# Gated cross-attention block with a mixture of experts: a matrix conversion put ahead of the register reads, pair weights and a bias put elsewhere

## The reference, cut to what matters

```python
x = x + tanh(g_ffn[0]) * ffn(layernorm(x))
# ffn, with normed = rmsnorm(...) * norm_weight
shared = relu(normed @ sw1 + sb1) @ sw2 + sb2          # 256 -> 1024 -> 256
probs = sigmoid(flat @ router_w.T)                     # 8 experts
scores, idx = top_k(probs, 2)
w = scores / (sum(scores) + 1e-6)
h = relu(einsum("td,edh->teh", flat, ew1) + eb1)       # 8 experts, same widths
eo = einsum("teh,eho->teo", h, ew2) + eb2
routed = einsum("teo,te->to", eo, comb)                # comb holds w at idx
return shared + routed
```

## Time and profile before

| | |
|---|---|
| median of 3 runs | 702.06 us (701.38 to 702.97) |
| the profiled execution, whole | 701.34 us |
| its span | 699.5 us |
| TensorE busy in matmuls | 598.9 us, 86% of the span |
| VectorE busy | 482.4 us, 69% |
| ScalarE busy | 392.8 us, 56% |
| GpSimd busy | 281.7 us, 40% |

### The profile page before, as it was taken

How to read it: one execution, slowest core, us unless ns; L and a number is a source line. 1 busy time by engine, 2 the same in 40 slices (tenths; PEclk the granted TensorE clock), 3 DMA queues, 4 the chain that set the end, 5 groups by cost and what they waited for, 6 DMA issues and landing times. The chain is left out here.

```text
span 699.5 us, 19174 instructions
## 1 busy us (share of the span) xinstructions
PE 598.9 (86%) x6150; PEld 499.4 (71%) x6150; DVE 482.4 (69%) x1298; ACT 392.8 (56%) x994; POOL 281.7 (40%) x327
## 2 busy tenths in 40 slices
PE   2689999999999999999757999898999999799960
PEld 2457777777777778777536887787788788587850
DVE  6858777877777877778695766547555556556537
ACT  4368888888888888887716423144352444424320
POOL 7303444443443334446530178605345525355120
PEclk9799999999999999999975999999999999999995
DMA  8536557775555555632040042203434332341218
GB/s 219 153 81 144 151 138 188 184 197 135 132 130 137 138 141 138 155 87 68 1 181 1 9 152 84 98 23 116 141 110 147 107 120 91 120 138 46 61 49 311
DMA packets 86601, 84.29 MB, mean 121 GB/s; under 512 B 17879, under 2 KB 80341, under 8 KB 86430
## 3 DMA queue, kind: packets, MB, share of 16 engines
q1 hardware_dynamic: 78686, 70.83, 36.8%
q0 software_dynamic: 2976, 8.16, 3.2%
q10 hardware_dynamic: 4896, 4.76, 2.5%
HBM read 55.43 MB, written 28.30 MB: 120 GB/s over the span
## 5 line engine op out<-in xcount | busy, mean ns | idle before, releaser
L925 PE MATMUL ps<-ident,probs 112*125 112x112 f32 x768 | 192.6, 277 | 2.5 <-POOL probs L508 1.4
L713 ACT ACTIVATE probs<-probs,negmax 112x375 f32<-112x375 f32 x256 | 154.9, 608 | 26.0 <-DVE negmax L1227 25.8
L1079 PE MATMUL ps<-w,arena 128*128 128x256 f16 x1152 | 139.0, 277 | 20.8 <-DVE arena L1370 20.6
L763 ACT ACTIVATE arena<-ps,b 128x256 f32<-128x256 f32 x192 | 78.5, 473 | 138.8 <-PE ps L1068 138.8
L925 PEld LDWEIGHTS ps<-ident,probs 112*125 112x125 f32 x768 | 138.9, 188 | 23.6 <-issue 7.4
L1227 DVE CUSTOM_DVE_ANT_0 probs<-ps,neg 112x375 f32<-112x375 f32 x256 | 137.3, 538 | 11.8 <-issue 9.5
L1079 PEld LDWEIGHTS ps<-w,arena 128*128 128x128 f16 x1152 | 109.9, 99 | 45.6 <-DVE arena L1370 32.2
L508 POOL TENSOR_TENSOR probs<-probs,gp_in 112x375 f32<-112x375 f32 x64 | 58.6, 915 | 181.2 <-ACT probs L713 181.1
L1234 DVE TENSOR_TENSOR arena<-ps,gpT 125x336 f32<-125x336 f32 x192 | 97.0, 506 | 46.3 <-PE ps L925 45.7
L1068 PE MATMUL ps<-probs,w 128*128 128x256 f16 x816 | 91.9, 273 | 0.0
L1068 PEld LDWEIGHTS ps<-probs,w 128*128 128x128 f16 x816 | 79.9, 98 | 9.2
(11 more groups left out here) (173 smaller groups left out, 829.8 us busy)
## 6 DMA issues: line engine op xcount, KB each, us to landing
k_scratch<-kT SPq DMA_DIRECT2D x96, 93.8 KB
kst<-k_scratch SPq DMA_DIRECT2D x64, 140.6 KB, 3.5
w1s<-in_L_ffn_ew_dram SPq DMA_DIRECT2D x8, 1024.0 KB, 4.9
w2s<-in_L_ffn_ew_dram SPq DMA_DIRECT2D x8, 1024.0 KB, 5.6
x_sent<-y_sb SPq DMA_DIRECT2D x12, 516.0 KB, 5.1
ctx_in<-in_ctx_dram SPq DMA_DIRECT2D x16, 375.0 KB
probs<-x_sent ACTq DMA_DIRECT2D x18, 258.0 KB, 2.6
arena<-y_back SPq DMA_DIRECT2D x7, 512.0 KB, 7.1
```

The lines of the kernel that those rows point to most:

```text
L713: act.activation(probs[:, n % PROBS], probs[:, n % PROBS], ACT.Exp, bias=negmax[:, p, n:n + 1], scale=-1.0, accum_out=rowsum[:, p, ORDER[n ...
L763: act.activation(hid32[:, f], ps[:, f // 2 % 4, f % 2 * TILE:(f % 2 + 1) * TILE], ACT.Relu, bias=b1[:, f, e:e + 1]).then_inc(h_relu, 1)
L925: mm = pe.transpose(ps[0:KP, PT[n % 2], c * S:(c + 1) * S], probs[:, n % PROBS, c * KP:(c + 1) * KP], ident[0:S, 0:S])
L1079: mm = pe.matmul(ps[:, 4 + a, 0:D], hid[:, u, f, a * P:(a + 1) * P], w2[:, p, w, f], start=(f == 0 and j == 0), stop=(f == NF - 1 and j == 2))
```

## The change

Three edits. In the experts' loops of ScalarE and VectorE the conversion of the next first matrix comes ahead of the register read; the start of an expert is taken from the register that held the end of the one before, so each of these two engines reads one register for each expert instead of two, and one more at the very start. TensorE and GpSimd read as before. The seven instructions for the pair weights go from the end of the shared expert to the place behind its tile 2 (`weigh_pairs`), and ScalarE's exponential from behind tile 6 to behind tile 1. The bias `sb2` is added in each shared tile, to its own 256 rows, between the split and the wait for the result, with a wait of VectorE for its own addition (`sb2_added`).

```diff
--- before.py
+++ after.py
@@ -203,6 +203,7 @@
             sem("cnt_made"), sem("rank_mm"), sem("slot_made"), sem("tiles_made"), sem("scattered"))
         in_w1, in_w2 = sem("in_w1"), sem("in_w2")
         in_b2 = sem("in_b2")
+        sb2_added = sem("sb2_added")
         w1_hi, w1_lo, w2_hi, w2_lo = sem("w1_hi"), sem("w1_lo"), sem("w2_hi"), sem("w2_lo")
         x_in = sem("x_in")
         xT_mm, xT_made = sem("xT_mm"), sem("xT_made")
@@ -773,19 +774,21 @@
 
             activate(0, E)
             split_high(1, 1)
-            with act.Fori(1, ST) as i:
-                activate(i, E)
+            activate(1, E)
             act.wait_ge(dve_ask, 4)
             act.activation(top[:, 6:8], top[:, 6:8], ACT.Exp, scale=-1.0).then_inc(act_gave, 1)
+            with act.Fori(2, ST) as i:
+                activate(i, E)
             take_tile(0)
             act.wait_ge(words_taken, 1)
             load_tile(1)
             act.wait_ge(tiles_made, 1)
+            end = act.value_load(tile_of[0:1, 0:1], min_val=0, max_val=RT)
             for e in range(E):
-                first = act.value_load(tile_of[0:1, e:e + 1], min_val=e, max_val=RT)
-                end = act.value_load(tile_of[0:1, e + 1:e + 2], min_val=e + 1, max_val=RT)
+                first = end
                 if e + 1 < E:
                     split_high(e + 2, e % 2)
+                end = act.value_load(tile_of[0:1, e + 1:e + 2], min_val=e + 1, max_val=RT)
                 with act.Fori(first, end) as r:
                     activate(r + ST, e)
                     take_tile(r + 1)
@@ -1377,11 +1380,25 @@
             def shared_tile(i):
 
                 split_hidden(i)
+                two = bass.ds(2 * i, 2)
+                dve.tensor_tensor(x_sb[:, two], x_sb[:, two], sb2_bc[:, :].unsqueeze(1).to_broadcast([P, 2, D]), ALU.add).then_inc(sb2_added, 1)
+                dve.wait_ge(sb2_added, i + 1)
                 for a in range(TILE // P):
                     dve.wait_ge(y_mm, 2 * i + a + 1)
                     row = bass.ds(2 * i + a, 1)
                     dve.scalar_tensor_tensor(x_sb[:, row].rearrange("p a d -> p (a d)"), ps[:, 4 + a, 0:D], gates[:, 1:2],
                                              x_sb[:, row].rearrange("p a d -> p (a d)"), ALU.mult, ALU.add).then_inc(y_made, 1)
+
+            def weigh_pairs():
+
+                dve.wait_ge(act_gave, 5)
+                then(dve.tensor_scalar(top[:, 6:8], top[:, 6:8], 1.0, None, ALU.add))
+                then(dve.reciprocal(top[:, 6:8], top[:, 6:8]))
+                then(dve.tensor_tensor(top[:, 8], top[:, 6], top[:, 7], ALU.add))
+                then(dve.tensor_scalar(top[:, 8], top[:, 8], 1e-6, None, ALU.add))
+                then(dve.reciprocal(top[:, 9], top[:, 8]))
+                then(dve.tensor_scalar(top[:, 9], top[:, 9], gates[:, 1:2], None, ALU.mult))
+                then(dve.tensor_tensor(top[:, 6:8], top[:, 6:8], top[:, 9].unsqueeze(1).to_broadcast([P, 2, NT]), ALU.mult))
 
             then(dve.tensor_scalar(sb2_bc[:, :], sb2_bc[:, :], gates[:, 1:2], None, ALU.mult))
             shared_tile(0)
@@ -1389,21 +1406,10 @@
             shared_tile(1)
             split_up_low(1, 1)
             shared_tile(2)
-
-            dve.wait_ge(y_made, 2 * 3 + 2)
-            then(dve.tensor_tensor(x_sb[:, :, :], x_sb[:, :, :], sb2_bc[:, :].unsqueeze(1).to_broadcast([P, NT, D]), ALU.add))
+            weigh_pairs()
             with dve.Fori(3, ST) as i:
                 shared_tile(i)
 
-            dve.wait_ge(act_gave, 5)
-            then(dve.tensor_scalar(top[:, 6:8], top[:, 6:8], 1.0, None, ALU.add))
-            then(dve.reciprocal(top[:, 6:8], top[:, 6:8]))
-            then(dve.tensor_tensor(top[:, 8], top[:, 6], top[:, 7], ALU.add))
-            then(dve.tensor_scalar(top[:, 8], top[:, 8], 1e-6, None, ALU.add))
-            then(dve.reciprocal(top[:, 9], top[:, 8]))
-            then(dve.tensor_scalar(top[:, 9], top[:, 9], gates[:, 1:2], None, ALU.mult))
-            then(dve.tensor_tensor(top[:, 6:8], top[:, 6:8], top[:, 9].unsqueeze(1).to_broadcast([P, 2, NT]), ALU.mult))
-
             dve.wait_ge(z_done, 16 * ZEROS)
             dve.wait_ge(in_b2, 16)
 
@@ -1414,11 +1420,12 @@
 
             take_words(0)
             dve.wait_ge(tiles_made, 1)
+            end = dve.value_load(tile_of[0:1, 0:1], min_val=0, max_val=RT)
             for e in range(E):
-                first = dve.value_load(tile_of[0:1, e:e + 1], min_val=e, max_val=RT)
-                end = dve.value_load(tile_of[0:1, e + 1:e + 2], min_val=e + 1, max_val=RT)
+                first = end
                 if e + 1 < E:
                     split_up_low(e + 2, e % 2)
+                end = dve.value_load(tile_of[0:1, e + 1:e + 2], min_val=e + 1, max_val=RT)
                 with dve.Fori(first, end) as r:
                     split_hidden(r + ST)
                     dve.wait_ge(words_taken, r + 1)
```

## The result

Median of 19 runs 699.66 us (696.65 to 701.92), against 702.06 us of 19 runs of the kernel before on the same chip (701.10 to 705.79): 2.4 us less, ratio 0.9957, 95% interval 0.9942 to 0.9972. The forecast was 694.2, with a range from 689.5 to 699.0, and the measured time lies outside it. The profiled execution took 701.35 us, 1.7 more than the median. That of the kernel before took 701.34, so the two traces show none of the gain that the median has.

A forecast was written before the change was run, and what follows sets the result against it. TensorE was taken as the bound, so only its idle time could be won, with the engines' ring setting the time in places. 701.34 - 2.9 (shared stage) - 5.0 (experts) = 693.4, forecast 694.2 on the median's scale; range 689.5 to 699.0.

The forecast's parts named there:

- The bias tile by tile: Shared expert, VectorE: each bias piece takes 0.7 us, hidden in 0.92 us of idle time waiting for TensorE.
- Expert 0's high half: ScalarE's first matrix conversion starts 2.3 us sooner from earlier row words and one read less, besides the shared stage's 2.9.
- Reads: Experts 1 to 6: the high half no longer waits for two register reads, 1.09 us sooner at each expert.
- the rival of reads that wait: Reads wait for their engine's running instruction, so 0.5 to 0.6 us come back per expert: 697.7 us, chance 0.06.
- the one that the order gives nothing: Something else fills the 1.27 us before the high half; only shared stage and 1.75 us stay: 697.4, chance 0.03.
- Tile 5: Shared stage: GpSimd freed sooner, so VectorE's split overlaps its matrix conversion in fewer slow pairs, 1.1 us less loss.
- the likeliest case: One scatter held, at expert 2: 694.2 us, own range 692.3 to 696.3, chance 0.40.
- the slower cases: All scatters held (704.2 us, chance 0.06) and half of something unseen (0.05); slower together given 0.07.
- My central case is one held scatter, at expert 2: GpSimd's second scatter held by VectorE's low half costs 2.8 + 1.1 us; the experts' lead ends at 5.0 us.
- two or three held, about 697, up to 700: Rival: more than one expert's scatter held, each further one costing about 3 us of the lead; chance 0.16.
- Expert 4 adds 1.1, because its low half and the load behind it are early: At expert 4, already held before the change, the high half's lead grows by 1.1 us.
- None held: Rival: no scatter held by a low half; shared stage gives 2.9 and experts 8.8, 690.4 us, chance 0.24.

The follow-up runs named there:

- the reads alone: Kernel before with only the expert loops' register reads moved behind the matrix; two runs, 716.03 us (ratio 0.9994) and 705.46 us (1.0015).
- cut and later load: Changed kernel with w1's low half made by four instructions and the next 1 MB load held behind the conversion's first cut: 686.84 us, ratio 0.9767.
- The shared part alone: Changed kernel with register reads as in the kernel before; three runs: 720.95, 718.60 and 696.91 us, ratios 1.0139, 1.0118 and 0.9904.
- the fill: Changed kernel with ScalarE's one read kept ahead of its matrix and 14 unused matmuls in TensorE's gap in expert 0: 695.42 us, ratio 0.9890.
- later load, second run: Changed kernel with the next expert's 1 MB load held behind the first cut of GpSimd's conversion, on a disturbed chip: 709.10 us, ratio 0.9994.
- third run: Changed kernel with the next expert's 1 MB load held behind the first cut of GpSimd's conversion, on an undisturbed chip: 687.91 us, ratio 0.9792.

## Why the prediction was wrong

**Right, by its own steps.** The bias tile by tile: 0.68 to 0.71 us in idle time, forecast 0.7 at no cost. The weights: 1.72 us (418.15 to 419.87) in the pause. Tile 3: 1.80 us back. Expert 0's high half 5.1 us earlier, forecast 2.9 + 2.3. Reads: 1.08 us at each expert, forecast 1.09, with nothing waiting for them; the rival of reads that wait is out, and so is the one that the order gives nothing (the high half did come forward by the two reads). Tile 5 gave 0.8 and not 1.1, so the shared stage 2.7 and not 2.9. One bound was added up wrongly: the shared stage's 0.9 to 3.6 us give 693.5 to 696.2 for the likeliest case, not 692.3 to 696.3. And the chances of the slower cases add up to 0.085, not 0.07.

**Wrong: the step "My central case is one held scatter, at expert 2".** It counted two ties, experts 1 and 5, as going well, and let the hold at 2 set expert 3 free. The runs showed the opposite order, for a reason that I had half in hand. Behind a hold, ring and scatters move together, and the distance is that of expert 5 before, 1.08 us, less the 1.08 of the reads: +0.01 to +0.02 us at experts 2 and 5, in the change's two profiles and in both of the reads alone. The scatter was never held there. Behind an expert *without* a hold, TensorE sets the scatter, and the low half comes first. That is expert 1 (behind 0) and expert 3 (behind 2). The change's first profile shows who is waited for ahead of the scatters of experts 1 and 2: VectorE's last piece of `y_sb` waits for TensorE's matmuls at 1, and at 2 VectorE waits for GpSimd's landing (line 616) before it writes `dest`:

```profile
488.68 0.42 DVE L1441 TENSOR_TENSOR y_sb<-ps,kst 128x256 f32<-128x256 f32 x1 [0.71 <-PE ps L1082]
...
515.04 0.16 DVE L1434 SCALAR_TENSOR_TENSOR dest<-words 128x2 int32<-128x2 f32 x1 [4.75 <-POOLq L616]
```

So holds come at every second expert, two and not one: the rival "two or three held, about 697, up to 700", to which I gave 0.16. The size of one was near. The lead fell by 6.1 + 1.1 - 2.7 = 4.5 at the first and 3.7 + 1.1 - 1.5 = 3.3 at the second, forecast 2.8 + 1.1 = 3.9. That the mean is 3.9 too is luck: the conversion came 3.3 and 3.4 us late, not 2.8, and the further 1.1 came at the first only, since expert 3 has three tiles.

**Wrong: "Expert 4 adds 1.1, because its low half and the load behind it are early".** It took 1.9. The early low half was ahead of the first scatter too, so the first was held, the second came behind it, and both landed beside the load, and the conversion came 12.04 us and not 9.48 behind the low half. I had written that nothing of this hurts at expert 4, and took the cost of its hold as fixed. Sum on the traces: 7.9 forecast, less 3.9 for the second hold and 3.0 for expert 4, leaves 1.0; 0.4 was left. The rest is pieces of 0.1 to 0.2, the hold at expert 6 among them, which the prediction did not see.

**Only argued, or open.** At expert 1 the clock seems to decide how far the low half is ahead. In seven traces with the change's shared part and its reads, TensorE had a gap of 1.70 to 1.92 us in expert 0. In three its granted clock then fell to half (the change twice, cut and later load), and the low half was 0.98 to 0.78 us ahead. In four it did not, and the low half was between 0.21 us ahead and 0.01 behind. The shared part alone goes the same way: with a gap of 2.26 us each time, the low half was 0.94 and 0.99 us behind the scatter in the two traces whose clock stayed up, and 0.28 in the one whose clock fell. One trace with the fill supports it as a cause; why the clock falls in one execution and not in another stays open. Open too is why the median gained 2.4 us where the profiled execution gained nothing; I had no trace of a faster execution of this kernel. "None held", forecast 690.4, didn't occur by itself; with the landings moved out of the load's way the change was worth 10.0 us, forecast 11.7. And all of this holds for undisturbed chips; the change as a whole was not timed on the two others, where its shared part alone was a loss.

The Trainium skill (SBUF — State Buffer, "Who interferes with whom") says that the one of the two engines that issues second blocks. Every scatter here that began over 45 ns behind a low half agrees. The other way round the traces don't agree: at expert 2 of the change the low half began 0.01 us behind a scatter of 0.96 us, and took 2.31 us instead of 2.29. VectorE did not wait for the scatter's end.

## What to carry to other kernels

When a step in a ring of engines is made earlier, look at what it overtakes, at each passage and by the engine that sets the time there, and not at one passage for all: a distance of 0.8 us shorn of 1.1 changed who came first at every second expert, and that took more than the 1.1 gave. Ask then what the delayed work runs into, since one hold cost next to nothing until the transfer behind it fell beside a 1 MB load. And an edit that looks for nothing but time should be measured part by part: the shared part alone (0.990 of before) did more than the whole change (0.996 and 0.998) on undisturbed chips, and one wait on SyncE turned the reads from a loss (an expert stage of 212.3 us instead of 207.6) into a gain (199.7 instead of 204.6).

## What the runs showed of the hardware

- A GpSimd scatter held by a VectorE low half ends 0.84 us after it, whatever the point at which it began (1.90 to 3.07 us instead of 0.96). Some 45 ns decide: with the low half 0.04 us ahead (later load, second run, expert 1) the scatter took 0.96, with 0.05 us ahead (the same run, expert 6) 3.07, and with 0.08 us ahead (third run, expert 2) 3.05.
- The clock fell after a gap of 1.70 us in one execution and not in another. In the changed kernel's first profile, the gap and what followed, and the granted clock:

```profile
470.23 0.83 PE L1082 MATMUL ps<-w,arena 128*128 128x256 f16 x6 [1.70 <-DVE arena L1373]
471.29 6.43 PE L1082 MATMUL ps<-w,arena 128*128 128x256 f16 x42 [0.23 <-DVE arena L1373]
```

```profile
471.30:475.00 3.70, 3.70 (x19) 2.59 (x20) 2.72 (x7) 0.00 (x0) 1.43 (x2) 0.54 0.56 224
```

  and in the later load's third run, behind a gap of 1.71 us:

```profile
468.40:472.00 3.60, 2.90 (x23) 1.88 (x24) 3.46 (x9) 0.33 (x1) 0.40 (x1) 1.00 0.00 0
```

  0.54 is near the lower of the two levels, 1.2 GHz of 2.4; 48 such matmuls take 5.40 us at the full clock, so 42 take 4.7.
- A held scatter's rows landed 5.2 us after its end beside a 1 MB load, and 1.6 to 2.2 us after it without one.
- A register read of one number took 0.28 us and ran beside the long instruction of its own engine.
- On two chips TensorE stood idle with no releaser shown, and at half clock, while GpSimd issued its `x_sent` scatters; single tiles of 10.8 us took 15 to 42. The cause isn't known.
